# Gated attention beside a mixture of experts on one core: fp32 value products and a half swap by transfer

## The chip, the cores and the metric

The kernel runs on one core of a Trainium2 chip. The metric is the device time of one execution in microseconds (us); of several runs the median is given. TensorE (PE) multiplies matrices, VectorE (DVE), ScalarE (ACT) and GpSimd (POOL) do elementwise work, and SyncE (SP) issues transfers, as ACT and POOL also do.

## The reference

The input x has 8 blocks of 512 tokens with 128 features. It is normalized once (first rows, xn); attention normalizes again (second rows), and both attention and the experts add to x:

```python
xn = _layernorm(x, axis=-1)
x = x + attention(xn, ...) + experts(xn, ...)

# attention, x here is xn
xn = (x - mu) / jnp.sqrt(var + EPS) * ln_w + ln_b
uv = jax.nn.silu(xn @ uv_w.T + uv_b)
u, v, base = (uv[..., :E], uv[..., E:2 * E], uv[..., 2 * E:])      # E = 256, base has 128
base = base[:, :, None, :] * gamma[None, None] + beta              # two of them: q and k
base = _rope(base)                   # [x1*cos - x2*sin, x2*cos + x1*sin], x1 and x2 the halves
q, k = (base[:, :, 0, :], base[:, :, 1, :])
qk = jnp.einsum('bis,bjs->bij', q, k)
kernel = jnp.square(jax.nn.relu(qk / SQRT_S + bias[None]))
out = u * jnp.einsum('bij,bje->bie', kernel, v)
return out @ o_w.T + o_b + shortcut

# experts: squared-relu FFN, one shared and the best 2 of 8 by a sigmoid router
out = sq_relu(x_flat @ W_sh_up) @ W_sh_down
for e in range(E):
    out = out + combine[:, e:e + 1] * (sq_relu(x_flat @ W_up[e]) @ W_down[e])
```

## The kernel before

The kernel has four stages. A prologue loads and turns the weights, computes the statistics and the routing, and fills a buffer of 4680 KB in HBM with zeros (line 388). Then come eight turns, one per block of 512 tokens, in which attention and the shared expert are computed and each token's row is sent twice to the slots of its experts by GpSimd (line 865). Then 72 tiles of slots pass through the experts. At the end the rows that the experts returned are added and stored. The change touches the turns and the small part of the prologue that prepares block 0.

In the turns everything is held transposed, features on the partitions and tokens along a row. Each engine runs its instructions in the order in which they are written, and semaphores tie the engines together. `turn(b, first, last)` of each engine is that order, written out by hand; `sequence_turns` runs it for block 0, in a loop for blocks 1 to 6, and for block 7. A turn of block b works on block b and also prepares block b+1 (transposing its rows, its base) and finishes block b-1 (gate, output, mix).

Precise products are made from three fp32r matmuls: an operand is split into a high half, cast to fp32r by ACT, and a low half, the difference, computed by DVE. `product` (lines 906 to 910) multiplies high by low, low by high, high by high, accumulating in one PSUM bank. Operands of type fp32, without a split, are multiplied by one matmul instruction, as in `shared_down` (line 999) and `output` (line 1020).

The steps that matter, in the order in which data passes through them for block b+1: `second_norm` (DVE) makes the rows xs2; `second_rows_turned` (PE, line 976) transposes them into a bank; `second_rows_hi` (ACT, line 400) and `second_rows_lo` (DVE, line 638) make x2_hi and x2_lo. `base_part` (PE) multiplies them by the 128 base columns of the weights, and by the same columns with their halves swapped (BSW), into two banks, base and bsw. `base_silu` (ACT) applies Silu to both (line 409) into silu_b, then scales and shifts each of the two twice, for q and k (line 414), into base_qk. `rotate_base` (DVE, lines 711 and 714) multiplies the plain pair by the cosines (rot1) and the swapped pair by the sines (rot2), `rotate_sum` (line 720) adds them, ACT casts the sum to qk_hi (line 452), and `qk_split` (line 725) makes qk_lo. `first_norm` (line 613) makes the first rows, `first_rows_turned` transposes them, `first_rows_hi` and `first_rows_lo` (lines 403 and 642) split them for the shared expert. `scores` (PE) makes four tiles qk0 to qk3 of 128 keys by 512 queries; `kernel_square` (DVE) adds the bias (line 748) and squares the positive part (line 751) into kern, which holds two tiles. `kernel_hi` (ACT, line 443) and `kernel_lo` (DVE, line 757) split each of them. `v_part` (PE), `v_bias` (DVE, line 731), `v_silu` (ACT, lines 422 and 423: the same Silu twice, once cast to v_hi and once to fp32) and `v_split` (DVE, line 738) make v_hi and v_lo. `values` (PE) multiplies v and the kernel tile, two products of 128x512 per tile, eight per turn; `gate` (DVE, line 765) multiplies the result by u.

Four PSUM banks form a ring. RING lists the 16 uses per turn in order, each use takes the next bank, and `ring_free` lets TensorE wait for whoever reads the bank's previous contents. For the x2 transposes of the next block that is the reading of the four score tiles at line 748. SyncE issues the loads of the prologue and then nothing until it loads slots for the experts.

## Time and profile before

| | us |
|---|---|
| median of 3 runs | 454.58 |
| lowest and highest | 454.51, 455.42 |
| profiled execution | 456.13 |
| its span | 454.3 |
| mean granted TensorE clock, of full speed | 0.927 |

The profile comes from one execution, recorded by the hardware. Busy times over the span are: TensorE 371.5 us (82%) in 2041 matmul records, its weight loads 299.2, VectorE 294.0 (65%), ACT 245.2 (54%), GpSimd 176.2 (39%). TensorE's records overlap, because matmuls are pipelined and their ends are modelled; the distance from start to start tells more than the duration. Durations of other engines overlap their successors by some 0.1 us too. A bracket at the end of a row tells how long the engine had been idle before it and what ended that. Where PEclk is 1.00 TensorE ran at 2.4 GHz, at 0.50 at 1.2 GHz. "x_hi" and the like stand for several tiles whose numbers are left out.

### The profile page before, as it was taken

To read this page: it belongs to the slowest core of one execution; us is meant where nothing else is said; L and a number is where in the kernel's file an instruction comes from. 1 tells how busy PE (TensorE), PEld (TensorE's weight loads), DVE (VectorE), ACT (ScalarE), POOL (GpSimd) and SP (SyncE) were. 2 spreads that over 40 slices of the span, in tenths; PEclk is the share of its full clock that TensorE was granted. 3 is DMA by queue.
4 is the path that set the end of the run, shared out by engine and by line. 5 is a ranking of instruction groups with operands and counts; after the bars stand their busy time and mean duration, and the time that the engine had idled before them with its cause. 6 is when DMAs were issued, how large, how long until landed. Compare 5 with 4: busy or idle time off the path is not lost.

```text
span 454.3 us, 8228 instructions
## 1 busy us (share of the span) xinstructions
PE 371.5 (82%) x2041; PEld 299.2 (66%) x2042; DVE 294.0 (65%) x726; ACT 245.2 (54%) x453; POOL 176.2 (39%) x159
## 2 busy tenths in 40 slices
PE   1168457799998989899999969999999999999800
PEld 1157435566665667566756638999999999999700
DVE  2889798988988888989899822333333333333245
ACT  0203027565676766665656715666666666666400
POOL 0486004562534526180716200444444444444500
PEclk9995567999999999999999997999999999999955
DMA  8618993000000001010100101221222212212089
GB/s 227 212 46 237 231 191 61 29 30 19 23 23 18 29 6 41 0 47 0 41 6 30 42 0 30 66 63 60 64 59 63 64 57 65 64 57 65 36 251 309
DMA packets 49792, 33.65 MB, mean 74 GB/s; under 512 B 5747, under 2 KB 46195, under 8 KB 49780
## 3 DMA queue, kind: packets, MB, share of 16 engines
q1 hardware_dynamic: 29120, 16.27, 12.8%
q10 hardware_dynamic: 16308, 8.26, 9.1%
q0 software_dynamic: 4352, 8.99, 5.5%
q8 instruction: 5, 0.08, 0.1%
q14 instruction: 7, 0.06, 0.0%
HBM read 17.63 MB, written 15.87 MB: 74 GB/s over the span
## 4 chain that ended last, share of the span: by engine, by line
PE 50%; DVE 21%; issue 12%; ACT 6%; ACTq 4%; DMA 4%; DVEq 2%; POOL 0%; POOLq 0%
PE bank L1133 14%; PE bank L1114 7%; PE bank L908 7%; PE bank L909 6%; PE bank L910 6%; DVE work L748 3%; PE bank L1020 3%; ACT base_qk L414 3%; DVE xs L613 3%; ACTq L356 2%; PE bank L946 2%; PE bank L1107 2%; DMA work<-results 2%; DVE qk_lo L725 2%; DVE k_lo L757 2%
## 5 line engine op out<-in xcount | busy, mean ns | idle before, releaser
L865 POOL DMA_INDIRECT slots_in<-xs,slot_now x64 | 75.2, 1176 | 124.5 <-DVE xs L634 77.9
L895 POOL DMA_INDIRECT results<-work x72 | 69.2, 960 | 109.2 <-DVE work L822 107.4
L822 DVE TENSOR_SCALAR work<-bank,work 128x128 f32<-128x128 f32 x72 | 25.2, 350 | 93.5 <-PE bank L1133 93.5
L1133 PEld LDWEIGHTS bank<-wdn,work 128*128 128x128 f32 x576 | 75.1, 191 | 6.0
L1133 PE MATMUL bank<-wdn,work 128*128 x576 | 75.7, 274 | 0.0
L499 ACT ACTIVATE work<-bank 128x512 f32<-128x512 f32 x72 | 43.1, 599 | 14.7 <-PE bank L1114 14.7
L505 ACT ACTIVATE work<-bank 128x512 f32<-128x512 f32 x72 | 43.1, 598 | 8.9 <-PE bank L910 3.4
L1114 PE MATMUL bank<-cst,work 128*128 128x128 f32 x288 | 43.9, 276 | 0.0
L908 PE MATMUL bank<-wup_lo,x_hi 128*128 x72 | 35.3, 491 | 1.0 <-DVE x_lo L813 1.0
L493 ACT CAST x_hi<-bank 128x128 fp32r<-128x128 f32 x72 | 19.0, 266 | 30.8 <-PE bank L1107 30.8
L1114 PEld LDWEIGHTS bank<-cst,work 128*128 128x128 f32 x288 | 34.2, 143 | 0.5 <-issue 0.4
L751 DVE SCALAR_TENSOR_TENSOR work<-work 128x512 f32<-128x512 f32 x32 | 33.8, 1055 | 1.1
L908 PE MATMUL bank<-k_lo,v_hi 128*128 128x512 f32 x64 | 27.6, 431 | 6.1 <-DVE k_lo L757 6.1
L999 PE MATMUL bank<-work,shdn 128*128 128x512 f32 x64 | 30.0, 592 | 0.0
L909 PE MATMUL bank<-wup_hi,x_lo 128*128 x72 | 29.1, 404 | 0.0
L910 PE MATMUL bank<-wup_hi,x_hi 128*128 x72 | 28.8, 400 | 0.0
L748 DVE SCALAR_TENSOR_TENSOR work<-bank,bias_t 128x512 f32<-128x512 f32 x32 | 21.9, 684 | 8.9 <-PE bank L910 8.9
L813 DVE TENSOR_TENSOR x_lo<-bank,x_hi 128x128 fp32r<-128x128 f32 x72 | 20.9, 291 | 9.8 <-ACT x_hi L493 7.1
L910 PE MATMUL bank<-k_hi,v_hi 128*128 128x512 f32 x64 | 25.1, 393 | 0.0
L909 PE MATMUL bank<-k_hi,v_lo 128*128 128x512 f32 x64 | 25.0, 391 | 0.0
L434 ACT ACTIVATE work<-bank 128x512 f32<-128x512 f32 x32 | 18.2, 595 | 12.0 <-PE bank L999 12.0
L452 ACT CAST qk_hi<-work 128x1024 fp32r<-128x1024 f32 x8 | 8.4, 1049 | 28.9 <-DVE work L720 28.9
(177 smaller groups left out, 824.1 us busy)
## 6 DMA issues: line engine op xcount, KB each, us to landing
slots_in<-spare ACTq DMA_DIRECT2D x1, 4680.0 KB, 31.7
work<-slots_in SPq DMA_DIRECT2D x36, 130.0 KB, 2.2
x_all<-in_L_attn_x SPq DMA_DIRECT2D x4, 512.0 KB, 8.7
work<-in_L_ffn_W_up SPq DMA_DIRECT2D x4, 512.0 KB, 3.5
wdn<-in_L_ffn_W_down SPq DMA_DIRECT2D x4, 512.0 KB, 7.3
work<-results SPq DMA_DIRECT2D x8, 256.0 KB, 7.2
work<-results ACTq DMA_DIRECT2D x8, 256.0 KB, 7.7
out<-x_all SPq DMA_DIRECT2D x8, 256.0 KB, 5.7
```

The lines of the kernel that those rows point to most:

```text
L499: act.activation(hid_t[:, h, :], P_HT[h][:, :], ACT.Square).then_inc(hid_t_made, 1)
L505: act.activation(hid[:, h, :], P_UP[h][:, :], ACT.Relu).then_inc(relu_done, 1)
L748: dve.scalar_tensor_tensor(kern[:, j % 2, :], ring(f"qk{j}")[:, :], float(S) ** -0.5, bias_t[:, at:at + T], ALU.mult, ALU.add).then_inc(ke ...
L751: dve.scalar_tensor_tensor(kern[:, j % 2, :], kern[:, j % 2, :], 0.0, kern[:, j % 2, :], ALU.max, ALU.mult).then_inc(kern_made, 1)
L865: pool.indirect_dma_start(slots_in, bass.IndirectOffsetOnAxis(slot_now[:, k, t:t + 1], 0), xs1[:, k, t, :], None).then_inc(tokens_sent, 16)
L895: pool.indirect_dma_start(results, bass.IndirectOffsetOnAxis(dest[:, at:at + 1], 0), slot_y[:, k, :], None).then_inc(returned[k], 16)
L908: pe.matmul(dst, w_hi, m_lo, start=start, stop=False)
L909: pe.matmul(dst, w_lo, m_hi, start=False, stop=False)
L910: return pe.matmul(dst, w_hi, m_hi, start=False, stop=stop)
L999: pe.matmul(P_OUT[:, :], shdn[:, c, :], sh[:, c % 2, :], start=(c == 0), stop=False).then_inc(shdn_done, 1)
L1114: last = pe.transpose(P_HT[h][:, c * P:(c + 1) * P], hid[:, h, c * P:(c + 1) * P], ident)
L1133: last = pe.matmul(P_Y[h][:, 0:D], hid_t[:, h, rows], wdn[:, of, c, :].rearrange("p a d -> p (a d)"), start=(c == 0), stop=(c == HC - 1))
```

## The change

The value products take v and the kernel tiles as they are, in fp32, with one matmul each, and v_hi, v_lo, k_hi, k_lo go with the instructions that made them; the kernel tile now has room for all four tiles of a block. The second base product and its Silu go too. In their place SyncE copies the two halves of silu(base), 64 partitions of 512 fp32 each, crosswise within SBUF with two transfers per block, and ACT scales the swapped half after a wait for them. On ACT, `base_scaled` is now a function of its own behind `first_rows_hi`. The ring has 15 uses, and `ring_before` finds the previous use of a bank.

```diff
...
         xs2, xs1, spare = sb("xs2", [P, TB, D]), sb("xs1", [P, TOPK, TB, ROW_W]), sb("spare", [P, TB, D])
         x2_hi, x2_lo = sb("x2_hi", [P, T], F32R), sb("x2_lo", [P, T], F32R)
         x1_hi, x1_lo = sb("x1_hi", [P, T], F32R), sb("x1_lo", [P, T], F32R)
-        v_hi, v_lo = sb("v_hi", [P, TB, EU], F32R), sb("v_lo", [P, TB, EU], F32R)
+        v = sb("v", [P, TB, EU])
         qk_hi, qk_lo = sb("qk_hi", [P, 2, T], F32R), sb("qk_lo", [P, 2, T], F32R)
-        k_hi, k_lo = sb("k_hi", [P, 2, T], F32R), sb("k_lo", [P, 2, T], F32R)
         g = sb("g", [P, 2, T])
+        kern = sb("kern", [P, TB, T])
         cos_sin = sb("cos_sin", [P, 2, T])
         base_qk = sb("base_qk", [P, 2, 2, T])
         bias_t = sb("bias_t", [P, BIAS_W])
...
             return stage[:, r % 2, k * H:(k + 1) * H].rearrange("p (c d) -> p c d", c=HC)
 
 
-        RING = ["x2", "base", "bsw", "x1", "v0", "v1", "sh0", "sh1", "u0", "u1", "qk0", "qk1", "qk2", "qk3", "sh2", "sh3"]
+        RING = ["x2", "base", "x1", "v0", "v1", "sh0", "sh1", "u0", "u1", "qk0", "qk1", "qk2", "qk3", "sh2", "sh3"]
         NRING = len(RING)
 
+        RING_BANK = [at % 4 for at in range(NRING)]
+
         def ring(name):
-            return banks[RING.index(name) % 4]
+            return banks[RING_BANK[RING.index(name)]]
+
+        def ring_before(at):
+
+            for back in range(1, NRING + 1):
+                if RING_BANK[(at - back) % NRING] == RING_BANK[at]:
+                    return RING[(at - back) % NRING], back <= at
 
         P_AV, P_OUT, P_FIN = banks[4:6], banks[6], banks[7]
 
...
                 sp.dma_start(wdn[:, e:e + 2], w_down[e:e + 2].rearrange("e (c p) d -> p e c d", p=P)).then_inc(ld_wdn, 16)
 
 
+            with sp.Fori(0, B) as b:
+                sp.wait_ge(silu_b_made, b + (START + 1))
+                sp.wait_ge(base_made, b * 4 + START)
+                sp.dma_start(silu_b[0:HALF, 1, :], silu_b[HALF:S, 0, :]).then_inc(bsw_landed, 16)
+                sp.dma_start(silu_b[HALF:S, 1, :], silu_b[0:HALF, 0, :]).then_inc(bsw_landed, 16)
+
             sp.wait_ge(tokens_sent, 16 * TOPK * NT)
             sp.wait_ge(base_made, START + B * 4)
             n_pairs = SLOT_TILES // 4
...
             def base_silu(b):
                 act.wait_ge(qk_made, START + b)
                 act.wait_ge(base_made, START + b * 4)
-                for n, name in enumerate(("base", "bsw")):
-                    act.activation(silu_b[:, n, :], of_ring(name, b), ACT.Silu, bias=uvbias[:, 2 + n:3 + n])\
-                       .then_inc(silu_b_made, 1)
+                act.wait_ge(bsw_landed, 32 * b)
+                act.activation(silu_b[:, 0, :], of_ring("base", b), ACT.Silu, bias=uvbias[:, 2:3]).then_inc(silu_b_made, 1)
+
+            def base_scaled(b):
                 for n, (by, plus) in enumerate(((gam, bet), (gam_sw, bet_sw))):
-                    act.wait_ge(silu_b_made, START + b * 2 + (n + 1))
+                    act.wait_ge(silu_b_made, START + b + 1)
+                    if n == 1:
+                        act.wait_ge(bsw_landed, 32 * (b + 1))
                     for k in range(2):
                         act.activation(base_qk[:, n, k, :], silu_b[:, n, :], ACT.Identity, bias=plus[:, k:k + 1], scale=by[:, k:k + 1])\
                            .then_inc(base_made, 1)
...
                     act.wait_ge(v_biased, START + b * 2 + (n + 1))
                     act.wait_ge(av_done, START + b * TB)
                     part = vf[:, 2 * n:2 * n + 2, :].rearrange("p t e -> p (t e)")
-                    act.activation(v_hi[:, 2 * n:2 * n + 2, :].rearrange("p t e -> p (t e)"), part, ACT.Silu)
-                    act.activation(part, part, ACT.Silu).then_inc(v_hi_made, 1)
+                    act.activation(v[:, 2 * n:2 * n + 2, :].rearrange("p t e -> p (t e)"), part, ACT.Silu).then_inc(v_made, 1)
 
             def u_silu(b):
                 act.wait_ge(g_made, START + b * 2)
...
             def shared_square(b, c):
                 act.wait_ge(sh_relu, START + b * HC + (c + 1))
                 act.activation(sh[:, c % 2, :], sh[:, c % 2, :], ACT.Square).then_inc(sh_made, 1)
-
-            def kernel_hi(b, j):
-                act.wait_ge(kern_made, b * TB + (j + 1))
-                act.wait_ge(av_done, START + b * TB + (j - 1) if j >= 2 else START + b * TB)
-                act.copy(k_hi[:, j % 2, :], kern[:, j % 2, :]).then_inc(k_hi_made, 1)
 
             def output_out(b):
                 act.wait_ge(out_acc, START + b + 1)
...
                 shared_square(b, 1)
                 if not first:
                     output_out(b - 1)
-                kernel_hi(b, 0)
-                kernel_hi(b, 1)
                 shared_relu(b, 2)
                 shared_relu(b, 3)
                 if not last:
                     second_rows_hi(b + 1)
                 shared_square(b, 2)
                 shared_square(b, 3)
-                kernel_hi(b, 2)
-                kernel_hi(b, 3)
                 if not last:
                     base_silu(b + 1)
                     first_rows_hi(b + 1)
+                    base_scaled(b + 1)
 
             second_rows_hi(0)
             act.wait_ge(uv_split, 1)
...
             base_silu(0)
             act.wait_ge(routed, 1)
             first_rows_hi(0)
+            base_scaled(0)
             sequence_turns(act, turn)
             output_out(B - 1)
 
...
                 dve.tensor_tensor(qk_lo[:, :, :], rot1, qk_hi[:, :, :].bitcast(F32), ALU.subtract).then_inc(qk_lo_made, 1)
 
             def v_bias(b):
-                dve.wait_ge(v_lo_made, START + b * 2)
+                dve.wait_ge(v_made, START + b * 2)
                 for n in range(2):
                     dve.wait_ge(ring_ready, START + b * NRING + (RING.index(f"v{n}") + 1))
                     dve.tensor_tensor(vf[:, 2 * n:2 * n + 2, :], ring(f"v{n}")[:, :].rearrange("p (t e) -> p t e", t=2),
                                       vb_bc[:, :].unsqueeze(1).broadcast_to([P, 2, EU]), ALU.add).then_inc(v_biased, 1)
 
-            def v_split(b):
-                part = "p t e -> p (t e)"
-                for n in range(2):
-                    dve.wait_ge(v_hi_made, b * 2 + (n + 1))
-                    dve.tensor_tensor(v_lo[:, 2 * n:2 * n + 2, :].rearrange(part), vf[:, 2 * n:2 * n + 2, :].rearrange(part),
-                                      v_hi[:, 2 * n:2 * n + 2, :].rearrange(part).bitcast(F32), ALU.subtract)\
-                       .then_inc(v_lo_made, 1)
-
             def kernel_square(b, j):
 
                 dve.wait_ge(ring_ready, START + b * NRING + (RING.index(f"qk{j}") + 1))
-                if j >= 2:
-                    dve.wait_ge(k_lo_made, b * TB + (j - 1))
+                if j == 0:
+                    dve.wait_ge(av_done, START + b * TB)
                 at = (TB - 1 - j) * P
-                dve.scalar_tensor_tensor(kern[:, j % 2, :], ring(f"qk{j}")[:, :], float(S) ** -0.5,
+                dve.scalar_tensor_tensor(kern[:, j, :], ring(f"qk{j}")[:, :], float(S) ** -0.5,
                                          bias_t[:, at:at + T], ALU.mult, ALU.add).then_inc(kern_biased, 1)
                 dve.wait_ge(kern_biased, START + b * TB + (j + 1))
-                dve.scalar_tensor_tensor(kern[:, j % 2, :], kern[:, j % 2, :], 0.0, kern[:, j % 2, :],
+                dve.scalar_tensor_tensor(kern[:, j, :], kern[:, j, :], 0.0, kern[:, j, :],
                                          ALU.max, ALU.mult).then_inc(kern_made, 1)
-
-            def kernel_lo(b, j):
-                dve.wait_ge(k_hi_made, b * TB + (j + 1))
-                dve.wait_ge(kern_made, b * TB + (j + 1))
-                dve.tensor_tensor(k_lo[:, j % 2, :], kern[:, j % 2, :], k_hi[:, j % 2, :].bitcast(F32), ALU.subtract)\
-                   .then_inc(k_lo_made, 1)
 
             def gate(b):
                 dve.wait_ge(out_acc, START + b)
...
                 qk_split(b)
                 kernel_square(b, 0)
                 kernel_square(b, 1)
-                v_split(b)
                 if not last:
                     second_norm(b + 1)
-                kernel_lo(b, 0)
-                kernel_lo(b, 1)
                 kernel_square(b, 2)
                 kernel_square(b, 3)
                 if not last:
...
                     first_norm(b + 1)
                 if not first:
                     mix(b - 1)
-                kernel_lo(b, 2)
-                kernel_lo(b, 3)
                 if not last:
                     rotate_base(b + 1)
                     first_rows_lo(b + 1)
...
                 at = RING.index(name)
 
                 reader = {"x2": (x2_lo_made, 1, 0), "x1": (x1_lo_made, 1, 0), "v0": (v_biased, 2, 0), "v1": (v_biased, 2, 1),
-                          "base": (silu_b_made, 2, 0), "bsw": (silu_b_made, 2, 1), "u0": (ut_made, 2, 0), "u1": (ut_made, 2, 1)}
+                          "base": (silu_b_made, 1, 0), "u0": (ut_made, 2, 0), "u1": (ut_made, 2, 1)}
                 for c in range(4):
                     reader[f"sh{c}"], reader[f"qk{c}"] = (sh_relu, 4, c), (kern_biased, 4, c)
-                read, per, k = reader[RING[at - 4]]
-                pe.wait_ge(read, START + b * per if at < 4 else START + b * per + (k + 1))
+                before, same_block = ring_before(at)
+                read, per, k = reader[before]
+                pe.wait_ge(read, START + b * per + (k + 1) if same_block else START + (b - 1) * per + (k + 1))
 
             def turned(name, b, made, rows):
                 pe.wait_ge(made, b + 1)
...
                     .then_inc(ring_ready, 1)
 
             def values(b, j):
-                pe.wait_ge(k_lo_made, b * TB + (j + 1))
+                pe.wait_ge(kern_made, b * TB + (j + 1))
                 if j == 0:
-                    pe.wait_ge(v_lo_made, START + b * 2 + 2)
+                    pe.wait_ge(v_made, START + b * 2 + 2)
                     pe.wait_ge(g_made, START + b * 2)
                 for e in range(2):
-                    last = product(P_AV[e][:, :], v_hi[:, j, e * P:(e + 1) * P], v_lo[:, j, e * P:(e + 1) * P],
-                                   k_hi[:, j % 2, :], k_lo[:, j % 2, :], start=(j == 0), stop=(j == TB - 1))
+                    last = pe.matmul(P_AV[e][:, :], v[:, j, e * P:(e + 1) * P], kern[:, j, :], start=(j == 0), stop=(j == TB - 1))
                 last.then_inc(av_done, 1)
 
             def output(b):
...
             def base_part(b):
                 pe.wait_ge(x2_lo_made, START + b + 1)
                 uv_part("base", b, BASE)
-                uv_part("bsw", b, BSW)
 
             def turn(b, first, last):
                 v_part(b, 0)
```

## Rows read from the trace of the kernel before

**Rows 1.** Busy time by stage; columns: window, length, then per engine, clock, DMA.

```profile
77.50:250.04 172.54, 158.11 (x664) 110.00 (x665) 154.60 (x272) 113.64 (x196) 78.39 (x68) 1.00 0.07 23
```

**Rows 2.** Waits, 102 to 262; waiting engine, line, releaser: us, times, longest.

```profile
PE bank L908 <- DVE k_lo L757: 5.8, 7, 0.9
```

**Rows 3.** Timeline of TensorE, one turn; columns: start, duration, engine, line.

```profile
151.42 0.49 PE L908 MATMUL bank<-qk_lo,qk_hi 128*128 128x512 f32 x1
...
151.75 0.39 PE L909 MATMUL bank<-qk_hi,qk_lo 128*128 128x512 f32 x1
151.98 0.40 PE L910 MATMUL bank<-qk_hi 128*128 128x512 f32 x1
...
159.58 0.49 PE L908 MATMUL bank<-k_lo,v_hi 128*128 128x512 f32 x1
...
162.04 0.66 PE L976 MATMUL bank<-cst,xs 128*128 128x128 f32 x4 [0.81 <-DVE work L748]
...
164.09 0.50 PE L908 MATMUL bank<-x_lo,uvw_hi 128*128 128x512 f32 x1
...
165.59 0.60 PE L976 MATMUL bank<-cst,xs 128*128 128x128 f32 x4
...
176.09 0.49 PE L908 MATMUL bank<-qk_lo,qk_hi 128*128 128x512 f32 x1
```

**Rows 4.** Timeline of VectorE, the same turn.

```profile
153.14 2.16 DVE L751 SCALAR_TENSOR_TENSOR work<-work 128x512 f32<-128x512 f32 x1
...
163.35 0.69 DVE L638 TENSOR_TENSOR x_lo<-bank,x_hi 128x512 fp32r<-128x512 f32 x1 [0.64 <-ACT x_hi L400]
...
164.24 1.11 DVE L613 TENSOR_SCALAR xs<-x_all,neg_mean,inv 128x128 f32 x4
...
169.41 1.23 DVE L714 TENSOR_TENSOR work<-base_qk,cos_sin 128x1024 f32<-128x1024 f32 x1 [0.18 <-ACT base_qk L414]
```

**Rows 5.** Timeline of ACT, the same turn.

```profile
165.30 1.27 ACT L409 ACTIVATE work<-bank,uvbias 128x512 f32<-128x512 f32 x2
...
167.86 1.51 ACT L414 ACTIVATE base_qk<-work,bet_sw,gam_sw 128x512 f32<-128x512 f32 x2
```

**Rows 6.** Groups of instructions by line, 76 to 265 us.

```profile
L757 DVE TENSOR_TENSOR k_lo<-work,k_hi 128x512 fp32r<-128x512 f32 x32 | 20.7, 685 | 0.2 <-ACT k_hi L443 0.2
```

**Rows 7.** Timeline of TensorE in the last turn.

```profile
258.08 0.47 PE L908 MATMUL bank<-k_lo,v_hi 128*128 128x512 f32 x1
...
264.52 1.88 PE L999 MATMUL bank<-work,shdn 128*128 128x512 f32 x4
...
266.23 1.88 PE L1020 MATMUL bank<-g,ow 128*128 128x512 f32 x4
```

**Rows 8.** Slot loads: the page's part on transfers, and the issues of line 327.

```profile
work<-slots_in SPq DMA_DIRECT2D x36, 130.0 KB, 2.2
...
L327 SPq DMA_DIRECT2D work<-slots_in x36: 367/373/472, 253.6 to 416.1; - x36
```

**Rows 9.** Timelines of ACT, VectorE and TensorE around block 0's start.

```profile
67.51 1.27 ACT L409 ACTIVATE work<-bank,uvbias 128x512 f32<-128x512 f32 x2
...
71.90 0.59 ACT L403 CAST x_hi<-bank 128x512 fp32r<-128x512 f32 x1 [0.32 <-PE bank L976]
...
72.15 1.22 DVE L714 TENSOR_TENSOR work<-base_qk,cos_sin 128x1024 f32<-128x1024 f32 x1
...
74.03 0.50 PE L908 MATMUL bank<-x_lo,shup_hi 128*128 128x512 f32 x1
...
77.50 0.51 PE L908 MATMUL bank<-qk_lo,qk_hi 128*128 128x512 f32 x1
```

**Rows 10.** Busy time by stretch in the prologue, columns as in rows 1.

```profile
59.90:63.60 3.70, 0.00 (x0) 0.00 (x0) 3.29 (x13) 0.58 (x1) 0.00 (x0) 0.96 1.23 200
63.60:67.40 3.80, 2.93 (x6) 1.82 (x6) 3.53 (x11) 1.19 (x1) 0.00 (x0) 0.50 1.25 156
```

**Rows 11.** Timeline of GpSimd, one turn.

```profile
153.55 1.19 POOL L872 TENSOR_TENSOR x_all<-x_all,xs 128x512 f32 x1
```

12 lines of the change are left out of this document (5 added, 7 removed).

## The prediction

> **What bounds the kernel now.** I read the busy times by stage first [rows 1]: in the seven turns between the first score product of block 0 (77.50) and that of block 7 (250.04), TensorE is busy 158.1 of 172.5 us and VectorE 154.6. Neither share says which of the two sets a turn, so the waits come next, then the timelines of one turn. Of TensorE's waits the longest is that for the low halves of the kernel tile (k_lo, line 757), 0.8 us per turn [rows 2]; as long is the one of the x2 transposes for VectorE's reading of the fourth score tile (line 748), which stands in its own row. I measure a turn by two moments on TensorE: S, the first product of `scores` (151.42, then 176.09), and X, the first x2 transpose for the next block (162.04) [rows 3]. S to X is 10.62 us, X to S 14.05, a turn 24.67. From S to the first `values` product (S+8.16) TensorE works through; X then waits for VectorE. X to S hangs on a chain: transposes, x2_hi, x2_lo, base product, Silu, scaling, second rotation (rot2, line 714, at 169.41 = X+7.37), then x1_lo, gate, rotation sum, split, S [rows 3 to 5]. From the start of rot2 to S are 6.68 us, nearly all VectorE work, which the change leaves as it is.
>
> **Parts, S to X.** On VectorE two v_lo and four k_lo subtractions go, each 0.60 us from start to start (685 ns with overlap) [rows 6]; four of the six, 2.4 us, lie ahead of the reading that X waits for (the fourth tile, before as after), so VectorE would allow X at S+8.2. On TensorE a product of three fp32r matmuls costs 3 x 0.23 = 0.69 us (151.75 to 151.98) [rows 3]. A raw fp32 product of 128x512 leaves two records; four records, two products, fill 264.52 to 266.23, so 0.86 us each [rows 7]. Raw is thus 0.17 us dearer per product, 1.3 us for the eight of a turn, against 0.69 saved on the second base product. `values(b,0)` begins to stream at 159.68 and takes 1.71: 161.4, S+9.98. TensorE is the later, so S to X is 9.98, a gain of 0.64 us per turn. The kernel tile's new wait on av_done costs nothing, since `gate(b-1)`, ahead of it in VectorE's order, waits for the same.
>
> **Parts, X to S.** The x2 transposes are through at X+0.5, `values(b,1)` takes 1.71, the base product starts at X+2.2 (now X+2.05 [rows 3]) and can be read 0.9 later. ACT no longer has two kernel copies ahead of the Silu, which starts there, at X+3.1, instead of 165.30 = X+3.26 [rows 5]; one of 0.68 us ends at X+3.77. The dropped second base product gives TensorE nothing here: line 613 has the first rows ready only at 165.35, so the x1 transposes can start at X+3.4, now X+3.55 [rows 3, 4]. Then come the two transfers. No copy from SBUF to SBUF is in the trace. The nearest row is the slot load, 130 KB from HBM on the same queue, 2.2 us to landing, 0.37 us of issue [rows 8]. So D, from the end of the Silu to the second landing, is 0.15 us to wake SyncE (my allowance), 0.40 for the first issue and 2.2 for the second: 2.75. Its bounds are 1.6, if a copy that touches no HBM lands a microsecond sooner, and 3.6, if the two pass one behind the other at half width (the first rival). I take 2.75, that row's value. Under it hides the unswapped half: x1_hi, now ahead of the scaling on ACT, ends near X+4.6, the first scaled pair (1.4 us) at X+6.0. The swapped half is scaled from 0.05 after the landing, rot2 follows the start of that by 1.55 (167.86 to 169.41 [rows 4, 5]): rot2 is at X+3.77+D+0.05+1.55 = X+5.37+D = X+8.12, but never before X+7.5, where ACT's own order sets it. S comes at X+14.80, a loss of 0.75 us.
> Who stands behind that wait: VectorE's x1_lo, and TensorE's `shared_up` for it. x1_lo is made at X+9.9, TensorE gets there at X+10.5 (3.4 to the x1 transposes, 0.6 for them, 3.4 for two `values`, 1.7 for shared_down, 1.4 for v_part), so 0.6 us cover it. The u products wait for v_bias, made X+12.8 and X+13.4, and end at X+14.2, again 0.6 us before S. Only `scores` is late.
> A turn is 9.98 + 14.80 = 24.78 us, +0.11; seven turns +0.8 us; with D at its bounds -3.6 and +6.7.
>
> The Trainium skill bears on D: SBUF — State Buffer, in its part on the DMA ports of partition ranges, says that partitions 0..63 reach only eight of the sixteen ports, some 218 GB/s, and that two concurrent transfers on the two halves bring next to nothing over one. With the fixed 2 us of that page D would be an estimated 3.35 us and seven turns +5.0, the kernel near 464 us. No row here shows a transfer over 64 partitions.
>
> **Parts, the first block.** `base_silu(0)` runs at 67.51. Its scaling now stands behind `first_rows_hi(0)`, which waits for the x1 transposes and starts at 71.90 [rows 9]. So the first pair is scaled from 72.5, the second from 73.9, and rot2 starts at 75.4 instead of 72.15: S moves by 3.3 us, all exposed, since the 5.35 us behind rot2 stay. The swap, issued near 68.3 beside the zero fill (156 GB/s just before [rows 10]), has 5.5 us and stays hidden at twice the slot load's time; past 73.9 it costs one for one. TensorE ends v_part at 74.1 as now, then idles 3 us until x1_lo (77.2). After a like idle stretch (59.9 to 63.6) the granted clock fell from 2.4 to 1.2 GHz and stayed there through the next work [rows 10]. Should it fall here, 12 matmuls take 0.46 instead of 0.23 us, 2.8 more, of which 0.8 are covered: 0 to 2.0, I take 0.8. First block: +4.1 us (3.3 to 5.3).
>
> **Parts, the last block.** From 258.20 to 264.52 `values` runs with a stall for k_lo in it [rows 7]; four times 1.71 is 6.84 and gives 265.05: +0.55 us, on the path, with gate and output behind it. The seven ACT passes that go (four copies, two v Silus, one base Silu) are off the path but for the 0.16 us above. The experts' 183 us aren't touched.
>
> **Sum:** +4.1 +0.8 +0.55 = +5.4 us. The profiled execution took 456.13 us with a span of 454.3; its like would be 461.5. Against the median of the runs, 454.58, it is 460.0.
>
> **Rivals.**
> (1) The transfers don't overlap and run at half width: D 3.3 to 3.6. Seven turns cost 7 x (5.37+D-7.37-0.64), 4.6 to 6.7, the total 464 to 466. For it: nothing in the trace moves over 64 partitions. Against: the slot load takes 2.2 us in all for as many bytes as one of them.
> (2) A short D. At 2.1 or less ACT's order binds, a turn is 24.67+0.13-0.64 = 24.16, seven give -3.6; with a start of 3.3 and 0.55 the result is 454.8: no change.
> (3) Faster: TensorE's own work sets the turn. With rot2 at X+6.6, S would follow TensorE at X+13.3 and a turn last 23.3, -1.4 each: 454.6-9.8+4.1+0.55 = 449.4. It decides from D = 1.2 us, with an ACT that has the first pair done by X+5.0. For it: VectorE, the fuller engine by its waits, loses 3.6 us of work per turn. Against: x1_hi ahead of the scaling, and the slot load's 2.2.
> (4) VectorE's split is held by GpSimd. Beside GpSimd's addition (153.55, 1.19 us [rows 11]) an instruction with both inputs in SBUF took 2.16 us instead of 0.69 [rows 4]; in the new order it is off the path, which has 1.8 us of slack there. The addition starts near X+16 and the qk split (line 725, two SBUF inputs, on the path) ends by X+14.7. If GpSimd's sends, less disturbed, ended 1.5 us sooner, the two would meet: +1.5 per turn, 470.
>
> **Chances.** My forecast, 457.5 to 463: 0.57; (1) 0.20; (2) 0.10; (3) 0.08; (4) 0.05. The range takes in (1) and part of (2): 455.6 to 465.5. About 0.2%, 0.9 us, is what a measurement of this kernel can tell from no change. Faster 0.08 (case 3), same 0.10 (case 2), slower 0.82 (the rest).
>
> **What would show it.** In the changed kernel's timeline: turns (S to S) of 24.8 us with S to X 10.0; TensorE idle 1.4 us before `scores`, ended by qk_lo, and not idle before `values`; VectorE idle some 1.5 us before line 714's rotation, released by ACT and ACT by the transfer; D by SyncE's issues and landings; the first S near 81.6; `values` at 0.86 us per product. The prediction is wrong if D is far from 2.75, if that pitch is another, or if S of block 0 stays near 77.5.

## The result and the profile after

The changed kernel takes 459.5 us (median of 4 runs, 459.27 to 461.39), against 454.58 us (454.51 to 455.42) before: 1.0113 times as long, with a 95% interval of 1.0084 to 1.0142. The profiled execution took 459.53 us with a span of 457.7 (before 456.13 and 454.3). The forecast was 460.0 in a range of 455.6 to 465.5. Executions come in a faster and a slower state, and ratios with their intervals, here and below, compare only the faster ones; of all runs reported here one, of 465.07 us with the filler, was a slow one.

The top of the page of the changed kernel: the busy times of the engines, then the shares of the chain that ended last.

```profile
PE 376.6 (82%) x1953; PEld 284.9 (62%) x1954; DVE 253.7 (55%) x678; ACT 217.3 (47%) x397; POOL 173.0 (38%) x159
...
PE 69%; DVE 11%; issue 6%; DMA 5%; ACTq 4%; ACT 3%; DVEq 1%; POOL 0%; SPq 0%; POOLq 0%
```

Before, VectorE had 21% of this chain and TensorE 50%; VectorE has lost much work and shows less in the chain, yet the kernel is slower. The busy times of the seven turns, columns as in [rows 1]; the last three numbers are the clock, the DMA share and GB/s:

```profile
82.25:254.03 171.78, 160.11 (x589) 95.50 (x587) 119.94 (x230) 89.12 (x144) 71.40 (x64) 1.00 0.11 32
```

In seven turns VectorE is busy 34.7 us less than in [rows 1] (5.0 per turn: six subtractions of 0.6, and 1.35 of a wait inside an instruction, of which more below), ACT 24.5 us less. The stretch is 0.8 us shorter. It starts 4.75 us later (82.25 against 77.50), and that is where the time goes.

One whole X to S in the changed kernel, first TensorE; columns are start, duration, engine, line, operation and, in brackets, the idle time before it and what ended it.

```profile
163.04 1.88 PE L1002 MATMUL bank<-kern,v 128*128 128x512 f32 x4
164.75 0.60 PE L965 MATMUL bank<-cst,xs 128*128 128x128 f32 x4
...
168.06 0.66 PE L965 MATMUL bank<-cst,xs 128*128 128x128 f32 x4 [0.26 <-DVE xs L620]
168.56 3.60 PE L1002 MATMUL bank<-kern,v 128*128 128x512 f32 x8
171.99 1.88 PE L988 MATMUL bank<-work,shdn 128*128 128x512 f32 x4
...
177.87 0.51 PE L896 MATMUL bank<-x_lo,uvw_hi 128*128 128x512 f32 x1 [1.18 <-issue]
...
179.74 0.49 PE L896 MATMUL bank<-qk_lo,qk_hi 128*128 128x512 f32 x1 [0.20 <-issue]
```

The turn began with S at 154.93; X is 164.75 (S+9.82), and the next S 179.74 (X+14.99). Before X there is no idle time: TensorE's own `values` set it. Eight records of `values` fill 168.56 to 171.99, four products at 0.86 us. In [rows 3] the same X stood behind a wait for VectorE.

Then SyncE, ACT and VectorE in the same stretch:

```profile
168.63 0.46 SPq L331 DMA_DIRECT2D work<-work  x1
169.14 0.60 SPq L332 DMA_DIRECT2D work<-work  x1
```

```profile
167.84 0.69 ACT L421 ACTIVATE work<-bank,uvbias 128x512 f32<-128x512 f32 x1 [0.81 <-PE bank L898]
168.76 0.59 ACT L415 CAST x_hi<-bank 128x512 fp32r<-128x512 f32 x1 [0.23 <-PE bank L965]
169.24 1.52 ACT L429 ACTIVATE base_qk<-work,bet,gam 128x512 f32<-128x512 f32 x2
171.51 1.52 ACT L429 ACTIVATE base_qk<-work,bet_sw,gam_sw 128x512 f32<-128x512 f32 x2 [0.76 <-DMA work<-work]
```

```profile
173.07 1.23 DVE L721 TENSOR_TENSOR work<-base_qk,cos_sin 128x1024 f32<-128x1024 f32 x1 [1.05 <-ACT base_qk L429]
...
177.14 1.28 DVE L738 TENSOR_TENSOR work<-bank,vb_bc 128x512 f32<-128x512 f32 x2
178.34 1.27 DVE L732 TENSOR_TENSOR qk_lo<-work,qk_hi 128x1024 fp32r<-128x1024 f32 x1
```

The Silu ends at 168.53 and the swapped half starts at 171.51; with the 0.05 us that the prediction puts between the landing and that start, D is 2.93 us. ACT waits 0.76 us for it, VectorE 1.05 for ACT, and rot2 (now line 721) starts at X+8.32, where [rows 4] has it at X+7.37. Behind it all is as before: 6.67 us to S, against 6.68.

Last, the start of block 0: TensorE and ACT, and the busy times of four stretches.

```profile
73.69 0.41 PE L898 MATMUL bank<-uvw_hi,x_hi 128*128 128x256 f32 x1
76.97 0.80 PE L896 MATMUL bank<-x_lo,shup_hi 128*128 128x512 f32 x1 [2.86 <-DVE x_lo L649]
77.56 0.63 PE L897 MATMUL bank<-x_hi,shup_lo 128*128 128x512 f32 x1
...
82.25 0.63 PE L896 MATMUL bank<-qk_lo,qk_hi 128*128 128x512 f32 x1
```

```profile
67.26 0.69 ACT L421 ACTIVATE work<-bank,uvbias 128x512 f32<-128x512 f32 x1
71.64 0.59 ACT L415 CAST x_hi<-bank 128x512 fp32r<-128x512 f32 x1 [3.69 <-PE bank L965]
72.12 1.52 ACT L429 ACTIVATE base_qk<-work,bet,gam 128x512 f32<-128x512 f32 x2
73.54 1.51 ACT L429 ACTIVATE base_qk<-work,bet_sw,gam_sw 128x512 f32<-128x512 f32 x2
```

```profile
73.90:76.90 3.00, 0.21 (x1) 0.00 (x0) 2.81 (x4) 1.15 (x2) 2.39 (x3) 0.50 0.14 44
76.90:80.00 3.10, 3.04 (x7) 2.46 (x8) 3.10 (x5) 1.61 (x3) 2.49 (x3) 0.50 0.13 43
80.00:83.00 3.00, 3.00 (x8) 2.33 (x8) 0.44 (x1) 2.65 (x5) 2.36 (x4) 0.50 0.16 50
83.00:86.00 3.00, 3.00 (x14) 2.39 (x14) 2.37 (x4) 1.22 (x3) 0.90 (x1) 0.97 0.07 22
```

From the Silu to S are 14.99 us; before it was 9.99 (67.51 to 77.50 [rows 9]). ACT has nothing to do from 67.95 to 71.64, though the unswapped half lies ready: it waits for the x1 transposes. The second pair then follows the first without a wait for the transfers. The clock is granted at 0.50 (1.2 GHz) in the whole stretch from 73.9 to the first S, and each of the twelve matmuls of `shared_up` and `u`, but for the first (0.59), takes 0.43 us from start to start.

The whole account of the two traces, after less before: the prologue up to the Silu -0.25; Silu to first S +5.00; the first turn -1.52 (24.57 to 23.05); six turns +0.76; from the last S to `output` +0.51 (16.19 to 16.70). That is +4.5, and the experts' first transpose is indeed 4.48 us later (271.39, 275.87). Then 1.1 us come back, and the span ends 3.4 us longer.

### The profile page after: what moved, and what is told of

It is laid out like the page before. It is cut to its first block, busy times and chain, and to the rows that moved or that the text cites. A ratio compares the mean times of both kernels' runs of the same rounds, so it can differ in the third digit from the quotient of the medians.

```text
span 457.7 us, 7917 instructions
## 1 busy us (share of the span) xinstructions
PE 376.6 (82%) x1953; PEld 284.9 (62%) x1954; DVE 253.7 (55%) x678; ACT 217.3 (47%) x397; POOL 173.0 (38%) x159
## 4 chain that ended last, share of the span: by engine, by line
PE 69%; DVE 11%; issue 6%; DMA 5%; ACTq 4%; ACT 3%; DVEq 1%; POOL 0%; SPq 0%; POOLq 0%
PE bank L1120 13%; PE bank L896 9%; PE bank L897 8%; PE bank L1002 8%; PE bank L898 8%; PE bank L1101 7%; PE bank L988 5%; PE bank L1008 3%; ACTq L368 2%; DMA work<-results 2%; PE bank L1094 2%; PE bank L929 2%; PE bank L965 2%; PE bank L934 2%; ACT base_qk L429 2%
## 5 line engine op out<-in xcount | busy, mean ns | idle before, releaser
L853 POOL DMA_INDIRECT slots_in<-xs,slot_now x64 | 72.1, 1126 | 131.0 <-DVE xs L641 85.3
L1002 PE MATMUL bank<-kern,v 128*128 128x512 f32 x128 | 58.6, 593 | 0.0
L1002 PEld LDWEIGHTS bank<-kern,v 128*128 128x128 f32 x128 | 22.7, 190 | 20.6 <-issue 20.6
L747 DVE SCALAR_TENSOR_TENSOR kern<-bank,bias_t 128x512 f32<-128x512 f32 x32 | 21.9, 684 | 11.6 <-issue 8.4
L750 DVE SCALAR_TENSOR_TENSOR kern<-kern 128x512 f32<-128x512 f32 x32 | 23.1, 723 | 1.1
L896 PE MATMUL bank<-x_lo,uvw_hi 128*128 128x512 f32 x24 | 11.8, 493 | 13.0 <-DVE work L738 4.9
## 6 DMA issues: line engine op xcount, KB each, us to landing
slots_in<-spare ACTq DMA_DIRECT2D x1, 4680.0 KB, 29.6
```

The source lines that it names most:

```text
L853: pool.indirect_dma_start(slots_in, bass.IndirectOffsetOnAxis(slot_now[:, k, t:t + 1], 0), xs1[:, k, t, :], None).then_inc(tokens_sent, 16)
L896: pe.matmul(dst, w_hi, m_lo, start=start, stop=False)
L1002: last = pe.matmul(P_AV[e][:, :], v[:, j, e * P:(e + 1) * P], kern[:, j, :], start=(j == 0), stop=(j == TB - 1))
```

## The experiments

X, S, D and the parts of a turn are those of the prediction. A turn is given for the later blocks, where it is steady. Before, it is 24.67 (10.62 + 14.05), after 24.81 (9.83 + 14.98). Ratios are to the kernel before as measured beside each experiment, with medians of 454.8 to 455.2 us.

**Each part alone.** The first experiment keeps the raw value products and makes the swapped base by the second product and Silu, as before.

```diff
-                sp.dma_start(silu_b[0:HALF, 1, :], silu_b[HALF:S, 0, :]).then_inc(bsw_landed, 16)
-                sp.dma_start(silu_b[HALF:S, 1, :], silu_b[0:HALF, 0, :]).then_inc(bsw_landed, 16)
...
                 uv_part("base", b, BASE)
+                uv_part("bsw", b, BSW)
```

> One part alone: the raw fp32 value products, with the second base product and its Silu as in the kernel before and no transfer. My account: the first S stays near 77.4, S to X is 9.8 us in the turns (8.0 in the first), X to S stays at 14.05, so a turn lasts 23.9 instead of 24.67; with +0.5 in the last block the time is 448 us, below both kernels. Rival, that the dearer fp32 products are what costs: the time is that of the changed kernel, 459, or above.

Measured: 448.31 us (448.19 to 448.88), ratio 0.9862 (0.9842 to 0.9882). The turn is 23.82: 9.84 to X, 13.98 to S. From Silu to first S 9.99 us, as before. The first turn is 21.66. So the raw products are worth 0.85 us per turn, and 2.9 in the first. This version beats both kernels. Against it the changed kernel loses 0.99 us in each later turn, 1.4 in the first and 5.0 before the first S.

The second is the kernel before with the two transfers and ACT's new order, and the split value products left as they were. The rest of its edit (SyncE's two transfers, the wait for them, the ring of 15 uses) is that of the change.

```diff
-                uv_part("bsw", b, BSW)
...
                     first_rows_hi(b + 1)
+                    base_scaled(b + 1)
```

> The other part alone: the swap by two transfers, with the split fp32r value products of the kernel before. My account: first S near 82.2, S to X back at 10.6, X to S 15.1 (rot2 at X+8.4), a turn of 25.7; the time is about 466 us. Rival, that the transfers are harmless and the products cost: 455 to 456.

Measured: 460.26 us (458.51 to 460.74), ratio 1.0124 (1.0104 to 1.0145), not 466. The first S comes at 82.06 and X to S is 15.1, as expected; but S to X is 9.50 us instead of 10.6, from the second turn on. The timeline of VectorE shows why: the squaring of the kernel tile (line 771, line 751 before), which took 2.16 us in [rows 4], takes

```profile
158.66 0.90 DVE L771 SCALAR_TENSOR_TENSOR work<-work 128x512 f32<-128x512 f32 x1
```

GpSimd's addition [rows 11] no longer stands beside it, since VectorE and TensorE now come to this place 1 us later. I had left that out when I worked out 466. It gives back what the transfers cost in a turn: 24.6 against 24.67. That this kernel is slower all the same comes from its start: the first S is 4.56 us later, and the first turn, in which S to X is still 10.55, lasts 25.72 instead of 24.57. (The profiled execution is the fastest of the four, 458.51.)

**The transfers without their time.** The changed kernel with both halves scaled from the unswapped base and no transfer; ACT's order stays.

```diff
-                    if n == 1:
-                        act.wait_ge(bsw_landed, 32 * (b + 1))
...
-                        act.activation(base_qk[:, n, k, :], silu_b[:, n, :], ...
+                        act.activation(base_qk[:, n, k, :], silu_b[:, 0, :], ...
```

> The changed kernel without the two transfers and the wait for them; both pairs are scaled from the unswapped half, so the swap is left out of the computation. My account: ACT's own order sets rot2 at X+7.5 instead of X+8.3, X to S is 14.1, a turn 23.9, the first S unchanged near 82.2; the time is about 453.5. Rival, that TensorE's own work sets the turn: turns stay at 24.8 and the time at 459.5. Second rival, that rot2's place doesn't bind below X+8: 457 or so.

Measured: 453.99 us (452.88 to 455.56), ratio 0.9975 (0.9958 to 0.9992). The turn is 23.96, X to S 14.13. With the first experiment this splits the turn: raw products -0.85 (24.67 to 23.82), ACT's order, with the second base product and its Silu gone, +0.14 (to 23.96), the transfers +0.85 (to 24.81).

**What D is made of.** With the first transfer only (the swapped scaling reads the unswapped base, so that half of the swap is left out):

```diff
                 sp.dma_start(silu_b[0:HALF, 1, :], silu_b[HALF:S, 0, :]).then_inc(bsw_landed, 16)
-                sp.dma_start(silu_b[HALF:S, 1, :], silu_b[0:HALF, 0, :]).then_inc(bsw_landed, 16)
```

> The changed kernel with the first of the two transfers only; the second pair is scaled from the unswapped half but still waits for the transfer, so the swap is left out of the computation. If the two transfers pass one behind the other, as the first rival said, the one lands about 1.0 us sooner than the pair, near 1.9 us after the Silu; the scaling then goes by ACT's own order, rot2 at X+7.5, X to S 14.1 and a turn 23.95, as without any transfer. If they overlapped and only a fixed latency counted, the one would land 0.5 us sooner, rot2 at X+7.8, a turn 24.3.

Measured: 455.17 us in one run, turn 24.12, X to S 14.28. ACT:

```profile
166.31 0.69 ACT L420 ACTIVATE work<-bank,uvbias 128x512 f32<-128x512 f32 x1 [0.81 <-PE bank L897]
...
167.72 1.52 ACT L428 ACTIVATE base_qk<-work,bet,gam 128x512 f32<-128x512 f32 x2
169.30 1.52 ACT L428 ACTIVATE base_qk<-work,bet_sw,gam_sw 128x512 f32<-128x512 f32 x2
```

The second pair starts 1.58 us after the first instead of 1.42 (72.12 to 73.54 above, where nothing holds it), so the one transfer is just not hidden: D is 169.30 - 0.05 - 167.00 = 2.25 us. The second transfer adds 0.68 to that. Its issue stands 0.51 behind the first one's; its 131 KB at 200 GB/s are 0.66. To tell the two apart, the second is issued from ACT's queue, at the same time as the first:

```diff
-                sp.dma_start(silu_b[HALF:S, 1, :], silu_b[0:HALF, 0, :]).then_inc(bsw_landed, 16)
...
+                act.dma_start(silu_b[HALF:S, 1, :], silu_b[0:HALF, 0, :]).then_inc(bsw_landed, 16)
```

> The changed kernel with the second transfer issued by ACT right behind its Silu, so that both are issued at once. If D is set by the second issue, which stands 0.5 us behind the first on SyncE, the pair lands 0.5 us sooner, rot2 at X+7.85, a turn 24.35. If the bytes set it (262 KB at the 200 GB/s of the changed kernel's trace, 1.3 us), it lands at most 0.1 to 0.2 us sooner and ACT's issue (0.5 us) delays x1_hi: rot2 at X+8.1 to X+8.3, a turn of 24.7.

Measured: 459.79 us in one run, turn 24.68.

```profile
168.31 0.49 ACTq L423 DMA_DIRECT2D work<-work  x1
...
171.14 1.52 ACT L431 ACTIVATE base_qk<-work,bet_sw,gam_sw 128x512 f32<-128x512 f32 x2 [0.23 <-DMA work<-work]
```

The Silu ended at 168.28, so D is 2.81: issued 0.6 us sooner after the Silu (0.03 instead of 0.61), the second transfer lands 0.12 sooner. So the moment of its issue isn't what sets D. The changed kernel's own DMA windows (length, then busy times; the last number is GB/s) show nothing moving in the first microsecond after the issue at 168.63, then about 200 GB/s.

```profile
169.40:169.60 0.20, 0.20 (x2) 0.18 (x1) 0.00 (x0) 0.20 (x1) 0.20 (x1) 1.00 0.00 0
...
169.80:170.00 0.20, 0.20 (x2) 0.15 (x1) 0.00 (x0) 0.20 (x2) 0.20 (x1) 1.00 0.94 225
...
170.40:171.00 0.60, 0.60 (x3) 0.26 (x2) 0.21 (x1) 0.36 (x1) 0.34 (x1) 1.00 0.92 208
```

In finer windows the bytes of the pair move from 169.72 to 171.08, 1.36 us or 193 GB/s; the single transfer's took 0.74 us, 177 GB/s. The difference, 0.62, is nearly all of the 0.68 that the second one costs. With two queues the trace tells the transfers apart by queue, ACT's in 169.4 to 170.0 and SyncE's in 170.2 to 170.4 (packets, MB, share of the 16 engines):

```profile
q10 hardware_dynamic: 58, 0.12, 88.7%
...
q1 hardware_dynamic: 40, 0.08, 103.9%
```

They pass one behind the other, though their issues are 0.08 us apart. Here the pair needs 1.05 us, 250 GB/s, and its last bytes pass 0.33 us sooner after the Silu than in the changed kernel; but ACT goes on 0.64 us behind them instead of 0.43, so that only 0.12 is left. What the added 0.2 us behind the last byte are stays open.

The Trainium skill (SBUF — State Buffer, "Can I just issue two DMAs to hit both halves?") says that two concurrent transfers, on the two halves of the partitions, bring 6% over a single one, because they serialize. From one queue this case agrees: 193 GB/s against 177 for one alone are 9%. From two queues they serialize too, but at 250 GB/s. For one half of the partitions the page ("Door 1: The DMA port swizzle") gives some 218 GB/s at most; the 0.08 MB of SyncE's transfer in 0.2 us are 400, so that figure doesn't hold for it. Its roughly fixed 2 us per transfer ("The DMA setup-cost knee") is not borne out here either: D of the changed kernel is 1.2 us to the first byte, 1.36 of bytes and 0.4 to the landing, a fixed part of 1.6 with the wake-up of SyncE in it.

**Block 0.** The changed kernel with block 0's scaling moved back ahead of the wait for the routing and of x1_hi:

```diff
             base_silu(0)
+            base_scaled(0)
             act.wait_ge(routed, 1)
             first_rows_hi(0)
-            base_scaled(0)
```

> The changed kernel, with the scaling of block 0 on ACT ahead of its wait for routing and for the first rows. My account: the first S moves from 82.25 to between 78 and 80 and the turns behind stay at 24.8; the time is 455.5 to 457.5, the lower the sooner the swap lands beside the zero fill. Rival, that block 0's delay is the transfer beside the zero fill and not the order on ACT: the first S stays near 82.

Measured: 459.75 us (459.02 to 462.39), ratio 1.0124 (1.0085 to 1.0163): no gain. SyncE's first issue and ACT:

```profile
68.20 0.53 SPq L331 DMA_DIRECT2D work<-work  x1
```

```profile
68.12 1.52 ACT L429 ACTIVATE base_qk<-work,bet,gam 128x512 f32<-128x512 f32 x2
73.71 1.52 ACT L429 ACTIVATE base_qk<-work,bet_sw,gam_sw 128x512 f32<-128x512 f32 x2 [4.07 <-DMA work<-work]
```

The swapped half starts at 73.71, 5.6 us after the Silu's end at 68.09. What holds the transfers, by the traces, is the zero fill; no run leaves the fill out. These two lines of the DMA's share show 66 to 76 us in 40 slices of 0.25 us, first of this kernel, then of the changed one (9 is 90% busy or more):

```profile
DMA  9999999999999999999999999821000000000000
```

```profile
DMA  9999999974100997960000200000005200043000
```

In this execution the fill's packets go on until about 72.1. The transfers' first ones pass at 71.0, 2.8 us after the issue at 68.20 instead of 1.1, and their last near 73. In the profiled execution of the changed kernel the fill was done by 68.8, the transfers moved from 69.2 to 70.7, and ACT found them landed. With a late fill the swap lands between 73.6 and 74.6. So it did in four other profiled executions too: 5.9 us after the Silu's end with the split products, 6.1 with one transfer, 5.9 with two queues, 6.4 in the next experiment; in that of the gate, further down, the fill's packets ended at 71.4 and the swap was in time. The fill is late without any transfer too: from issue to landing it takes 29.6 us in the profile of the changed kernel, 31.7 in the kernel before and 31.7 to 33.6 in all the others. So the transfer is either well hidden or comes at the moment, or up to a microsecond behind, at which ACT's order has released it; it is one of two causes, each of which can hold block 0 by itself. From the Silu to the first S, in four profiled executions:

| | transfers | no transfers |
|---|---|---|
| scaling behind x1_hi | 14.99 (changed kernel) | 14.98 (no transfer) |
| scaling at once | 14.17 (this one, fill late) | 9.99 (raw only) |

**The clock in block 0.** Twelve matmuls into a bank that is free there, in the gap before `shared_up`:

```diff
                 v_part(b, 1)
+                if first:
+                    for _ in range(12):
+                        pe.matmul(P_FIN[:, :], x2_hi[:, 0:P], x2_hi[:, :], start=True, stop=True)
                 pe.wait_ge(x1_lo_made, START + b + 1)
```

> The changed kernel with twelve extra matmuls on TensorE in block 0 between v_part and shared_up, into a bank that nobody reads then. My account: they keep TensorE busy where it idled 2.9 us, the granted clock rises near 74 us instead of 83, shared_up and u run at 0.23 us per matmul, and the first S comes at 80.5 instead of 82.25; the time is 457.8. Rival, that the clock costs nothing here because the split on VectorE is the later: the first S stays near 82 and the time at 459.5.

Measured: 460.63 us (456.8 to 465.07 in nine runs), ratio 1.0107 (1.0074 to 1.0141). TensorE:

```profile
74.15 3.96 PE L1033 MATMUL bank<-x_hi 128*128 128x512 f32 x12
78.04 0.50 PE L896 MATMUL bank<-x_lo,shup_hi 128*128 128x512 f32 x1
78.38 0.39 PE L897 MATMUL bank<-x_hi,shup_lo 128*128 128x512 f32 x1
```

Behind the filler `shared_up` runs at 2.4 GHz (0.23 us from start to start instead of 0.43). The filler is no hindrance: rot2 comes at 76.16, since the transfers landed late (74.6), and x1_lo is made at 77.98. Rot2 to S is 5.40 us, as before (5.35), against 7.17 in the changed kernel. So the clock costs 1.8 us of block 0, and the filler takes them away; half of it went again to the later landing. From the Silu to S are 14.07 us instead of 14.99. In the time of the kernel none of this can be told: the ratio is that of the changed kernel, 1.0113, within the intervals.

**The new critical wait filled.** The changed kernel with VectorE's gate moved between the two rotations:

```diff
             def turn(b, first, last):
-                if not first:
-                    gate(b - 1)
                 rotate_sum(b)
...
+                if gated is not None:
+                    gate(gated)
                 dve.wait_ge(base_made, START + b * 4 + 4)
```

> The changed kernel with VectorE's gate moved from behind the rotation to the place between rot1 and rot2, where it idles 1.05 us for the transfer. My account, that the chain behind rot2 sets S: the gate is done from X+7.45 to X+8.65, rot2 starts at X+8.65, X to S falls from 14.97 to 14.1, a turn from 24.8 to 23.95, and the time to 453.5. Rival, that the gate has other waiters which then come late, or that TensorE sets the turn: turns stay at 24.8, 459.5.

Measured: 457.09 us (453.78 to 459.13), ratio 1.0043 (1.0019 to 1.0067). VectorE in the profiled execution (453.78 us):

```profile
169.74 1.29 DVE L760 TENSOR_TENSOR g<-bank,work 128x512 f32<-128x512 f32 x2 [0.34 <-issue]
170.94 1.22 DVE L723 TENSOR_TENSOR work<-base_qk,cos_sin 128x1024 f32<-128x1024 f32 x1
```

Rot2 follows the gate without a wait: the transfer is hidden under the gate, X to S is 14.3 to 14.5 and a turn 24.1 to 24.5 (expected 23.95). So the wait for the transfer is what the changed kernel's turn hangs on. Where X to S is 14.5, VectorE's v_bias waits 0.17 to 0.29 us for TensorE, which is the next limit. The median is 3.6 us above the expected 453.5, and the profiled execution is the fastest of the ten. The ten runs spread over 5 us, roughly with the mean granted clock, 459.1 at 0.912 and 453.8 at 0.928; what sets that clock from run to run I can't say.

**GpSimd's addition.** In the kernel before, it is moved ahead of `send(2)`, behind four of the eight sends, so that it misses the squaring:

```diff
                 send(0)
                 send(1)
+                add_rows(b)
                 send(2)
                 send(3)
-                add_rows(b)
```

> The kernel before, with one thing moved: GpSimd adds the rows to x (the instruction of 1.19 us, seen at X+16.2) after four of its eight sends instead of after all, near X+11. My account: the addition no longer meets VectorE's squaring of the first score tile, which takes 2.16 us beside it and 0.69 otherwise; S to X then falls from 10.62 to 9.5, as in the kernel with the swap alone, X to S stays at 14.05, a turn lasts 23.55 and the time is 447. Rival, that the long squaring isn't the addition's doing, or that S to X falls for another reason with the swap: turns stay at 24.67 and the time at 454.6. If the addition now holds VectorE's rotation sum or split instead, X to S grows by up to 1.2 and the turn stays as it was.

Measured: 458.22 us (457.7 to 460.15), ratio 1.0078 (1.0052 to 1.0103). S to X fell to 9.52 from the third turn on, as expected, but X to S rose to 15.43, so that a turn lasts 24.95. VectorE and GpSimd:

```profile
175.06 2.71 DVE L720 TENSOR_TENSOR work<-work 128x1024 f32<-128x1024 f32 x1
```

```profile
175.47 1.21 POOL L872 TENSOR_TENSOR x_all<-x_all,xs 128x512 f32 x1
```

Now the addition falls on the rotation sum, 2.71 us instead of 1.2, and that one is on the path. By the rows it starts 0.41 us before the addition and ends 1.09 after the addition's end (176.68), about its own length. The squaring of [rows 4] starts 0.41 before the addition of [rows 11] and ends 0.56 after it, again nearly its own length of 0.69. The Trainium skill (SBUF — State Buffer, "Who interferes with whom") says that a VectorE instruction with two SBUF inputs contends with a GpSimd instruction that reads SBUF, and that the order of issue decides who blocks. The contention is seen: VectorE's instruction gets next to nothing done beside the addition. The order doesn't agree, since in both pairs of rows VectorE's start is the earlier one; GpSimd's starts are rough in a profile, so that this stays open.

The same move in the first experiment's kernel:

```diff
                 send(1)
+                add_rows(b)
```

> The raw products alone (448.3 us), with the same move of GpSimd's addition. My account: with raw products TensorE's own work sets S to X at 9.84, so nothing is gained: turns of 23.8 and 448 us. Rival, that VectorE sets S to X there too: turns of 22.7, 440 us.

Measured: 450.27 us (448.98 to 451.7), ratio 0.9893 (0.9851 to 0.9935). S to X stays at 9.83, since TensorE sets it there, and X to S is 14.16 against 13.98. By its turns (23.82 against 23.99) the order of the first experiment stays the best; the intervals of the two ratios overlap.

## Why the prediction was right

**S to X.** Forecast 9.98, measured 9.83, TensorE the later and the pitch 0.86 us, all as the step had it. The raw products gained 0.79 us per turn instead of 0.64. What I hadn't weighed is that the whole gain of this part hung on one disturbed instruction: the second experiment shows that without any change to the products a squaring out of the addition's way gives 9.50. The gain of the raw products is measured against a kernel that loses 1.1 us there.

**X to S.** Forecast 14.80 with rot2 at X+8.12, measured 14.99 and X+8.32. The term that was mis-sized is D, 2.93 instead of 2.75 (0.18 us); with it, the step's own formula (X+5.37+D) gives X+8.30. The floor by ACT's order, X+7.5, gives X+14.18 for S; the kernel without transfers has 14.13. A turn came to 24.81 where I had 24.78.

**What D stood for.** The slot load gave 2.2 us from issue to landing for 130 KB. One transfer alone has nearly that (D 2.25 with the wake-up), so the row was a good model for one. The step added the second at the price of an issue (0.40). It costs 0.68, of which 0.62 are its bytes: the two don't overlap. In this rival (1) was right, and the step, which let them overlap, was not; that D came out so near was in part luck. The size of (1) was wrong: a D of 3.3 to 3.6 was not reached.

**Who waits.** I forecast 1.4 us of idle TensorE before `scores`. It is 1.38, but in two pieces: 1.18 before the u products and 0.20 before `scores`. The row of the first piece names "issue"; VectorE's line 738 (v_bias, two of 0.64 from 177.14) shows that its first half ends at 177.8, and the u products start at 177.87. They end 0.2 us before S where I had 0.6. The cover was thinner than I said, and S was not moved.

**The first turn.** Here the step failed. I took seven turns of +0.11; the first was -1.52. TensorE sets S to X there too, but it has less to do: in block 0 there is no `output` of a block before (1.71 us) and no transposes of it (0.44), and the first score products, at 1.2 GHz, cost 0.32 more. That makes 8.00 instead of 9.83 (7.69 in the first experiment, whose first score products run at 2.4 GHz), and TensorE works without a gap from S to X:

```profile
88.53 1.88 PE L1002 MATMUL bank<-kern,v 128*128 128x512 f32 x4
90.25 0.60 PE L965 MATMUL bank<-cst,xs 128*128 128x128 f32 x4
```

VectorE has read the fourth score tile at 89.26, S+7.0. In the kernel before, X of the first turn came as late as in the others (S+10.55), because VectorE was the later in both. The step took its start of `values(b,0)`, S+8.16, from a turn with an `output` in it and used it for all seven. VectorE's bound of S+8.2 was too late as well, by the 1.35 us of the disturbed squaring: in the steady turn it is through at S+6.9. Neither showed, since TensorE is the later in every turn.

**The first block.** Forecast +4.1, measured +5.0 from the Silu on. Silu to rot2 grew by 3.2 (4.64 to 7.82), which is the order's 3.3 as worked out. Rot2 to S grew by 1.8 (5.35 to 7.17), which is the clock, and I had 0.8: it was granted at 1.2 GHz throughout, within the bounds of 0 to 2.0 but near the far end. It didn't fall in the gap, as the step had it: `v_part` runs at 1.2 GHz in both kernels (0.21 us from start to start); in the kernel before the clock rises in its last two matmuls, in the changed one not before the first `scores`. "The swap stays hidden" held in the profiled executions of the changed kernel and of the one with the gate moved, and not in five others: it had 5.5 us, I allowed for twice the slot load's 2.2, and a late zero fill makes it 5.6 to 6.4. Removing the order alone gave 0.8 of the 5.0 us, removing the transfers alone nothing, both all of it.

**The last block.** Forecast +0.55, measured +0.51.

**The sum.** By parts: forecast 4.1 + 0.8 + 0.55 = 5.4; measured 4.75 - 0.76 + 0.51 = 4.5 up to the experts. In the experts' stage, which I left untouched, 1.3 us came back up to the fetch of the results (433.14 before, 436.29 after: +3.15 of +4.48). All of it comes back in the first six tiles: ACT's cast of a tile's rows is 4.18 us later for the first, 3.30 for the fourth, 3.09 for the seventh, and 3.07 near the end. The clock, by the windows from the kernel before and then the changed one, both around their first expert:

```profile
272.00:276.00 4.00, 3.16 (x9) 2.37 (x10) 1.08 (x6) 1.19 (x4) 0.00 (x0) 0.50 0.15 35
276.00:280.00 4.00, 4.00 (x20) 3.47 (x20) 0.89 (x5) 2.88 (x7) 0.00 (x0) 0.67 0.15 33
```

```profile
276.00:280.00 4.00, 3.28 (x12) 2.40 (x13) 1.08 (x6) 1.55 (x5) 0.00 (x0) 0.71 0.12 33
280.00:284.00 4.00, 4.00 (x27) 3.63 (x26) 1.08 (x6) 2.91 (x8) 0.00 (x0) 0.86 0.14 37
```

Both dip after the idle time between the stages; before, the clock reads 0.50 and then 0.67 in the first two stretches, after it 0.71 and 0.86. In windows of 1 us it is at 0.50 from 272 to beyond 278, after it only from about 278 to 281. That the 1.3 us are this dip is read from the windows and not shown by an experiment, and why it is shorter stays open. The medians differ by 4.9 us, more than the two profiled executions (3.4), because the one before was 1.5 above its median. So the sum was right in part by errors that cancel: against the parts, the first block cost 0.65 more, the first turn 1.6 less, the experts and the end 1.1 less, and the medians' difference is 1.5 more than that of the two profiles.

**The other rivals.** (2) and (3) needed a D of 2.1 or 1.2; with transfers of no length at all the turn is 23.96, not 23.3, for ACT's order binds first, as (3) granted. The range didn't hold all that the chances said of it: (1) reached to 466 and (2) was 454.8. (4), GpSimd on a VectorE instruction of the path, didn't happen in the changed kernel: the addition starts at 180.60, X+15.85, and the qk split ends at X+14.86. Its price was right: where the addition was moved up in the kernel before, the rotation sum paid 1.5 us for it.

## What to carry to other kernels

Two changes in one diff have two prices, and here they had opposite signs: the raw products alone make the kernel 1.4% faster (448.3 us), the transfers and the order that came with them turn that into 1.1% slower. A copy within SBUF that takes the place of 0.7 us of matmuls and 0.7 of activation must be hidden for 2.9 us; look for the work that lies between its issue and its reader, and put some there (the gate between the rotations took more than half of the loss away, a ratio of 1.0043 instead of 1.0113). And look at block 0 by itself in every sum: it has neither the covers nor the burdens of the others. Its start cost 4.75 us here, while the seven turns together were 0.8 us shorter than before.

## What the runs showed of the hardware that I had not expected

- Two transfers of 131 KB within SBUF, each from one half of the partitions to the other, move no bytes for 1.1 us after the first issue. Then they pass one behind the other, 262 KB in 1.36 us from one queue and in 1.05 from two; one alone takes 0.74. One lands 2.25 us after the end of the Silu before it, both 2.93, from two queues 2.81.
- Issued while a large fill on another queue is still under way, the same pair is scaled 5.6 to 6.4 us after the Silu, and one alone 6.1. With the fill late, its first packets pass some 2.5 to 3 us after the issue.
- A VectorE instruction with two SBUF inputs that meets GpSimd's addition runs, nearly all of it, behind it: 2.16 us instead of 0.69 (squaring), 2.71 instead of 1.2 (rotation sum). In the kernel before, this was 1.1 us of every turn; a shift of 1 us in the order of other work removes it or brings it to the path. A sum that moves such instructions against each other has an uncertainty of that size in it.
- Of two starts of block 0, both at 1.2 GHz up to the end of v_part, the one with 2.9 us of idle TensorE behind it stayed there to the first S; the other (raw only) had `shared_up` at 2.4 GHz from its second matmul on. The filler did the same for the changed kernel.
